# A pre-norm decoder layer on one core: the last batch's value and context products, and an older batch's residual, in another order

## What is computed

```python
x = x + attn(layernorm(x), wq, wk, wv, wo)      # 8 heads of 128, rms-normed and rotated q and k,
                                                # causal softmax
x = x + einsum('etf,efh->eth', gelu(einsum('eth,efh->etf', layernorm(x), ctx)), ctx)   # ctx: 375 rows a batch
x = x + ffn(layernorm(x), w1, b1, w2, b2)       # 256 -> 1024 -> 256, rounded to 8-bit grids, relu
```

## Time and profile before

| | |
|---|---|
| median of 3 runs | 654.48 us (654.33 to 656.54) |
| the profiled execution | 654.7 us |
| its span, first to last instruction | 652.9 us |
| busy in the span | PE 593.3 us (91%), DVE 588.1 (90%), ACT 543.0 (83%), POOL 348.0 (53%) |
| mean granted clock of TensorE | 0.974 of full |

### The profile page before, as it was taken

How to read it: one execution, slowest core, us unless ns; L and a number is a source line. 1 busy time by engine, 2 the same in 40 slices (tenths; PEclk the granted TensorE clock), 3 DMA queues, 4 the chain that set the end, 5 groups by cost and what they waited for, 6 DMA issues and landing times.

```text
span 652.9 us, 13103 instructions
## 1 busy us (share of the span) xinstructions
PE 593.3 (91%) x4624; PEld 477.3 (73%) x4624; DVE 588.1 (90%) x1339; ACT 543.0 (83%) x1402; POOL 348.0 (53%) x430
## 2 busy tenths in 40 slices
PE   1746889999999999999999999999999999997864
PEld 1424667777887788888778877888887788776753
DVE  3768899999999999999999999999999999998442
ACT  6675788999999999989998899999889999998522
POOL 1134555665555565666655555656666555556111
PEclk9967999999999999999999999999999999999978
DMA  8071566766776766667687676666677777666451
GB/s 296 0 200 36 114 139 138 137 138 150 149 148 137 147 133 142 141 141 153 133 151 152 143 152 138 137 142 132 143 149 138 150 152 146 134 141 138 89 109 37
DMA packets 222641, 88.92 MB, mean 136 GB/s; under 512 B 200704, under 2 KB 217552, under 8 KB 222320
## 3 DMA queue, kind: packets, MB, share of 16 engines
q1 hardware_dynamic: 222576, 88.08, 63.6%
HBM read 34.84 MB, written 3.67 MB: 59 GB/s over the span
## 4 chain that ended last, share of the span: by engine, by line
DVE 75%; ACT 9%; PE 5%; POOL 3%; issue 3%; DMA 3%; SPq 0%; ACTq 0%; DVEq 0%
DVE turn_s L433 11%; DVE turn_c L425 8%; DVE qk L524 8%; DVE o L550 5%; DVE ss L566 5%; DVE turn_c L614 5%; DVE ss L603 5%; DVE qk L639 4%; DVE h_t L590 2%; DVE y_out L545 2%; DVE g L628 2%; DVE x L634 2%; DVE stat L534 1%; POOL turn_c L354 1%; DVE xn L600 1%
## 5 line engine op out<-in xcount | busy, mean ns | idle before, releaser
L912 PE MATMUL psum<-wqkv,xT 128*112 128x512 f16 x384 | 148.3, 386 | 12.5 <-DMA xT<-xn 9.1
L913 PE MATMUL psum<-wqkv,xT 128*112 128x512 f16 x384 | 147.4, 384 | 0.0
L914 PE MATMUL psum<-wqkv,xT 128*112 128x512 f16 x384 | 147.1, 383 | 0.0
L354 POOL TENSOR_TENSOR turn_c<-turn_c,turn_s 112x1024 f32<-112x1024 f32 x32 | 75.7, 2365 | 48.4 <-DVE turn_s L433 48.4
L912 PEld LDWEIGHTS psum<-wqkv,xT 128*112 128x112 f16 x384 | 50.7, 132 | 43.4 <-DMA xT<-xn 9.7
L425 DVE TENSOR_TENSOR turn_c<-psum,cos_t 112x1024 f32<-112x1024 f32 x64 | 77.8, 1215 | 0.0
L433 DVE TENSOR_TENSOR turn_s<-psum,sin_t 112x1024 f32<-112x1024 f32 x64 | 77.7, 1214 | 0.0
L914 PEld LDWEIGHTS psum<-wqkv,xT 128*112 128x112 f16 x384 | 50.7, 132 | 34.1 <-issue 1.9
L922 PE MATMUL psum<-wo,oT 128*112 128x256 f16 x256 | 71.0, 277 | 4.7 <-DMA oT<-o 3.5
L524 DVE SCALAR_TENSOR_TENSOR qk<-turn_c,rms,qk 112x128 f16<-112x128 f32 x256 | 69.2, 343 | 2.6 <-ACT qk L796 2.5
L924 PE MATMUL psum<-wo,oT 128*112 128x256 f16 x256 | 71.0, 277 | 0.0
(11 more groups left out here) (107 smaller groups left out, 1699.2 us busy)
## 6 DMA issues: line engine op xcount, KB each, us to landing
ctxT<-in_ctx_cols SPq DMA_DIRECT2D x32, 375.0 KB, 3.4
ctx_in<-in_ctx_rows SPq DMA_DIRECT2D x32, 375.0 KB
x_in<-in_x SPq DMA_DIRECT2D x32, 112.0 KB, 2.3
out_y<-y_out SPq DMA_DIRECT2D x32, 112.0 KB, 2.9
w_raw<-in_w SPq DMA_DIRECT2D x2, 1024.0 KB, 6.1
w_raw<-in_wk SPq DMA_DIRECT2D x2, 512.0 KB, 5.0
w_raw<-in_wq SPq DMA_DIRECT2D x2, 512.0 KB, 6.5
w_raw<-in_wv SPq DMA_DIRECT2D x2, 512.0 KB, 8.2
```

Of the source, the lines that this page charges most:

```text
L354: pool.tensor_tensor(turn_c[:, 1, :], turn_c[:, 1, :], turn_s[:, 1, :], ALU.add).then_inc(k_turned, 1)
L912: pe.matmul(dst, hi, wqkv[:, 0, c, w, cols], start=c == 0, stop=False)
L913: pe.matmul(dst, hi, wqkv[:, 1, c, w, cols], start=False, stop=False)
L914: last = pe.matmul(dst, lo, wqkv[:, 0, c, w, cols], start=False, stop=c == MC - 1)
```

## The change

Three steps are moved, each for one turn near the end, and one wait is added where a move takes away what it followed from.

- Turn 29 on TensorE: `weigh_values(31)` is issued in the middle of the output projection of batch 30, behind `project_out3(30)`, instead of behind all of it.
- Turn 33 on VectorE: `residual_out(28)` goes ahead of `normalise_x2(31)`. Since `transpose_xn2(31)` could rely on `out_done(28)` for the order of these two, it now waits for `xn2_done(31)` as well.
- Turn 32 on TensorE: `ctx_out(31)` goes ahead of `out_units(29)`, with a wait for `g_done(31)` of its own.

No instruction is added or removed, and the programs of ScalarE, GpSimd and SyncE are the same.

```diff
 # VectorE, body
+                last_x2 = f.off == B - 1
                 if f.inside(B):
                     stats_x2(f)
+                    if last_x2:
+                        residual_out(i)
...
-                if i.inside(B):
+                if i.inside(B) and not last_x2:
                     residual_out(i)
 # TensorE
             def ctx_out(j):
                 pe.wait_ge(ctx_landed[j.off % SLOTS], landed(j))
+                if j.off == B - 1:
+                    pe.wait_ge(g_done, done(j))
...
             def transpose_xn2(j):
...
-                if j.off < 3:
+                if j.off < 3 or j.off == B - 1:
                     pe.wait_ge(xn2_done, done(j))
...
             def body(i):
...
+                last_ctx = e.off == B - 1
+                if last_ctx:
+                    ctx_out(e)
                 if g.inside(B):
                     out_units(g)
...
-                if e.inside(B):
+                if e.inside(B) and not last_ctx:
                     ctx_out(e)
...
+                last_values = b.off == B - 1
                 if c.inside(B):
                     project_out1(c)
                     project_out3(c)
+                    if last_values:
+                        weigh_values(b)
                     project_out2(c)
                     project_out0(c)
-                if b.inside(B):
+                if b.inside(B) and not last_values:
                     weigh_values(b)
```

## The result

| | before | changed |
|---|---|---|
| median of 15 runs | 654.48 us (652.95 to 656.73) | 656.68 us (655.27 to 658.81) |
| the profiled execution | 654.7 us | 656.47 us |
| its span | 652.9 us | 654.7 us |

The ratio of the two is 1.0031, 95% interval 1.002 to 1.0043: the change costs about 2 us. The forecast was 655.7 us, +1.2. The sign and the two larger terms came out as forecast; one term, step 2, did not, and the terms were also hidden under a second effect, so the table of the two profiles comes first.

A forecast was written before the change was run, and what follows sets the result against it. VectorE, 75% of the span, bounds most batches, but the last batch's chain sets the end. +0.40 - 0.33 + 1.33 - 0.21 = +1.19 us on 654.7 makes 655.9, given as 655.7 us, range 653.2 to 657.8.

The forecast's parts named there:

- step 2: Moving residual_out(28) ahead of normalise_x2(31) fits VectorE's idle time, so transpose_xn2(31) starts earlier: -0.33 us.
- Step 1: Value products of batch 31 come 1.32 us earlier, but invert_sums(31) waits behind residual_attention(30) on VectorE: +0.40 us.
- Step 3: With ctx_out(31) first, residual_ctx(31) still waits for out_units(29), residual_out(29) and add_b2(30): +1.33 us.
- Behind it: After quantise_x3(31), the clip's 0.21 us wait for the relu of batch 30 goes away: -0.21 us.
- The sum: The terms added, +1.19 us on the profiled execution's 654.7, 655.9; given as 655.7 us.
- The signs: What the changed trace would show: invert_sums(31) near 615.0, residual_ctx(31) released by add_b2(30), last clip waiting for nothing.
- the low clock at the last products: Longer TensorE gap before out_units(30) lowers the clock for hidden_units1(31) and out_units(31): +0.9 and +0.4 to 0.6, 657.1; chance 0.24.
- the collision: VectorE and GpSimd ports collide: normalise_x2(31) held for the 0.73 us of add_b2(29), 656.4; chance 0.06.
- The slower rival: Clock not back for batch 31's second block, until behind ctx_hidden(31): +4.3, 660.0; chance 0.05.
- The rival by which each move gives what TensorE gives: VectorE and GpSimd orders don't hold batch 31 back: -1.32, -0.33, -1.19, sum -2.84, 651.6; chance 0.05.

The follow-up runs named there:

- the clock kept full: The changed kernel with unread matmuls added where TensorE idles; 650.79 us, ratio 0.9932 to the kernel before.
- the last kernel: The changed kernel with batch 31's VectorE steps reordered, add_b2(29) held, a second x3b, one transpose wait less, and unread matmuls where TensorE idles; 649.07 us, ratio 0.9893.
- the pair of kept-busy kernels: The kernel before and the changed kernel, both with the same unread matmuls where TensorE idles; 648.95 us and 650.79 us.
- the kernel with all ties undone: The changed kernel with batch 31's VectorE steps reordered, add_b2(29) held, a second x3b and one transpose wait less, no unread matmuls; 650.54 us, ratio 0.9924.

## Why the prediction was right, and where it was not

**Step 1** (+0.40 by `residual_attention(30)` ahead of `invert_sums(31)`): right, 0.41 in the changed kernel and 0.40 with that move alone. That the order of VectorE, and not TensorE, was the cause is shown by the kernel that turns the two around.

**Step 2** (-0.33) failed. The residual did fit into VectorE's idle time, as priced, but the step went on "in the rows it is GpSimd that pays, and I price `normalise_x2(31)`, which now runs beside `add_b2(29)`, at its 0.41". It took 0.80 in the changed kernel, with the move alone and with the clock kept full, and 0.41 with `add_b2` held. The rows I read that from showed `split_o`, which reads two tensors and had started 0.01 us ahead of the add; there the add is the slower one, 1.80 us. Here the add starts first, by 0.07, and VectorE pays. The rival had the right engine and nearly twice the price, 0.73 where 0.39 was measured. The Trainium skill's page SBUF — State Buffer, section Who interferes with whom, would have been the better guide: whichever of the two engines issues first holds their shared ports for its whole instruction, and the other one is blocked. All the traces here agree on who pays, 0.39 us for VectorE and 1.07 for GpSimd, though not that the blocked one pays its whole time behind the other (last section). One execution turns the order of the same two operations around: in the last kernel, with all undone and kept busy, `split_o(30)` came 0.20 behind the add, and now `split_o` is the slower one, 1.60 instead of 1.22, and the add takes its usual 0.72. VectorE, then GpSimd:

```profile
603.36 1.60 DVE L557 TENSOR_TENSOR o<-on,o 112x1024 f16<-112x1024 f32 x1 [0.28 <-ACT o L729]
```

```profile
603.16 0.72 POOL L353 TENSOR_TENSOR x3b<-x,b_rows 112x256 f32<-112x256 f32 x1 [2.99 <-DVE y_out L552]
```

So it is the order that decides, in these traces. Another 0.10 is the second wait on the transpose, which I had counted as free. So -0.33 became +0.15.

**Step 3** (+1.33 by `residual_out(29)` and `add_b2(30)` behind the pair): right to the hundredth, 1.33 in the changed kernel, with 1.36 from the pair's end with that move alone, and down to 0.38 with a second x3b. The second wait of `ctx_out(31)` adds about 0.1 that I had not counted (0.14 us from the later event to the start, where it was 0.04).

**Behind it** (-0.21): -0.22.

**The sum**: with step 2 corrected, 0.40 + 0.15 + 1.33 - 0.21 + 0.10 = 1.77, and the pair of kept-busy kernels measured 1.84. The forecast of 1.19 was low by step 2's term (0.48) and by that second wait (0.10).

**The signs**: most came as written, but by one of them I was wrong: the stretches at the low clock were to differ by no more than the three steps together (1.40), and the pair alone differed by 1.44. So the two profiles could not decide how much was the change's; the two kernels kept busy did.

**The rivals**: the low clock at the last products was there (`out_units(31)` 1.97 us), but the reason I gave isn't shown: kernels whose gap had not grown had it too. The measured 656.68 lies nearer to this rival's 657.1 and to the collision's 656.4 than to my 655.7, so the number alone would not have told them apart. The low clock comes at a moment of its own in each execution. Behind 620 us the granted clock falls 12.8 us after the start of batch 30's projection in the kernel before, 13.3 us with the context product alone and 13.7 us with the residual alone, though the programs of these three are the same up to there. The Trainium skill, page TensorE: Matmul & The Clock Gate, Part 1, has such moments as not tied to the kernel's start, and these traces agree. The slower rival did not come; the clock was back by 629.6. The rival by which each move gives what TensorE gives is refuted as long as VectorE's order stays. Once that order is adapted it holds for the value products (3.30 instead of 4.61 us); for the context product `residual_ctx(31)` did follow `ctx_out(31)` directly, and nothing was gained by that alone.

## What to carry to other kernels

A step that is moved earlier on its own engine is worth what its reader gains, and the reader can stand in another engine's order: before a move, write down for the reader what stands directly ahead of it and when that is released, and move both or neither. A swap of two neighbours that wait for the same event does not end the pair earlier; it moves the wait from one reader to the other, and single buffers (here x3b) can turn two parallel chains into one. Where batches ran out here, idle time of TensorE was paid twice, once as idle time and once as a low clock on what followed; keeping it busy with unread matmuls gave 1%, three times what the change cost. And two single profiles can differ by more in the clock than by the change: compare the stretches, and where they differ in clock, make it equal in both.

## What was not expected of the hardware

- A VectorE `tensor_scalar` on float32 (112x256, one tensor read) beside a GpSimd `tensor_tensor` add of the same shape took 0.80 us instead of 0.41, and the add its usual 0.72; it ended 0.15 us behind the add in the changed kernel, with the residual alone and with the clock kept full. A VectorE `tensor_tensor` (two tensors read) (112x1024) that started 0.01 to 0.17 us ahead of the add kept its 1.22 us, and there the add took 1.64 to 1.80, ending 0.6 behind it; so it was in all but one of the meetings of the two in these traces. In that one it started behind the add, by 0.20, and took 1.60, and the add 0.72. The one that waits takes less behind the other's end than it takes alone (0.15 of 0.41, 0.59 of 0.73, 1.08 of 1.22). The same operation paid or did not pay by who came first; that rests on one meeting for the `tensor_tensor`, and the `tensor_scalar` was never seen to start first.
- A TensorE instruction with two waits started 0.14 to 0.15 us behind the later event, with one wait 0.04 to 0.05. Taking one away was part of the kernel with all ties undone, but there the transpose waited for `ctx_out(30)`, so its gain was not measured, and the wait was not tested by itself.
